# A graph network's edge counts: summed in PSUM banks per 16 targets and copied out by ScalarE, with differences at the end, and four smaller rearrangements

## What is computed

```
# layer 0: attention over edges, 8 relations, 4 heads
e = leaky_relu(el + er); alpha = softmax of e over the edges of a target
h = segment_sum(alpha * feat_src_e, edge_dst) + h_bias
# layer 1: two relations, messages depend on source node and relation alone
agg = segment_sum(edge_nn(S, W_rel[rel], b_rel[rel]), dst)
c = sigmoid(i) * tanh(g); hn = sigmoid(o) * tanh(c); three dense layers
# layer 2: two mean aggregations over the same edges
aggr = segment_sum(xp[src], dst) / max(cnt, 1)
# layer 3: for node n, the first 1875 edges' ends
out = softmax over heads of alpha(row[n], col[n]), times xt[col[n]], summed over heads
```

## Time and profile before

| | |
|---|---|
| median of three runs | 2126.85 us (2119.39 to 2128.66) |
| the profiled execution's own time | 2116.86 us |
| its span in the profile | 2115.1 us |
| PE busy | 1475.9 us (70%) |
| DVE busy | 1249.3 us (59%) |
| ACT busy | 666.2 us (31%) |
| POOL busy | 543.2 us (26%) |
| mean DMA rate | 106 GB/s |

### The profile page before, as it was taken

One profiled execution on the slowest core, in us unless ns is written; L12 is line 12 of the kernel. 1 busy time (PEld: TensorE's weight loads), 2 busy tenths in 40 slices (PEclk: granted clock), 3 DMA queues, 4 the chain that ended last, 5 costly groups with the idle time before them and its releaser, 6 DMA issues.

```text
span 2115.1 us, 20437 instructions
## 1 busy us (share of the span) xinstructions
PE 1475.9 (70%) x5426; PEld 764.4 (36%) x5426; DVE 1249.3 (59%) x2926; ACT 666.2 (31%) x1118; POOL 543.2 (26%) x517
## 2 busy tenths in 40 slices
PE   6598988677766565304777775989976589889630
PEld 3254654111111111103555554544433254644520
DVE  5221222889998888687666676520036677576705
ACT  1024764677665555200000000357732110010010
POOL 0003774677777777300000000000000000000031
PEclk9797556555555555555999998989987579999865
DMA  5924664465565565502677772000000000000021
GB/s 197 64 106 152 195 208 132 128 196 182 182 197 185 191 195 184 159 0 91 192 207 207 204 208 86 1 22 1 1 1 0 30 1 1 1 1 2 10 65 49
DMA packets 98133, 223.84 MB, mean 106 GB/s; under 512 B 32984, under 2 KB 57476, under 8 KB 97540
## 3 DMA queue, kind: packets, MB, share of 16 engines
q1 hardware_dynamic: 74084, 158.00, 23.8%
q0 software_dynamic: 23968, 64.77, 11.6%
HBM read 140.09 MB, written 82.63 MB: 105 GB/s over the span
## 4 chain that ended last, share of the span: by engine, by line
PE 48%; DVE 21%; issue 12%; POOL 12%; DMA 3%; DVEq 2%; ACT 1%; SPq 1%; POOLq 0%; ACTq 0%
PE bank L1580 14%; POOL arena L497 10%; PE bank L1519 10%; PE bank L1397 5%; DVE adjacency L936 5%; PE bank L1430 3%; PE bank L1416 3%; DVE arena L1193 2%; DVE arena L1001 2%; PE bank L1646 2%; PE bank L1564 1%; PE bank L1643 1%; SPq L363 1%; PE bank L1548 1%; DVE arena L930 1%
## 5 line engine op out<-in xcount | busy, mean ns | idle before, releaser
L497 POOL DMA_INDIRECT arena<-feat_table,arena x469 | 506.8, 1081 | 300.0 <-issue 138.3
L1467 PE MATMUL bank<-arena 128*128 128x480 f16 x586 | 319.6, 565 | 176.2 <-DVE arena L930 125.2
L565 ACT ACTIVATE arena<-bank 128x480 uint16<-128x480 f32 x586 | 307.9, 586 | 85.1 <-PE bank L1467 82.7
L505 POOL DMA_INDIRECT arena<-al_table,edge_ends x15 | 14.1, 942 | 1168.0 <-DMA al_table<-arena 1163.7
L1580 PE MATMUL bank<-arena 128*128 128x472 f16 x1440 | 294.3, 368 | 9.9 <-DVE arena L1151 5.9
L1519 PE MATMUL bank<-arena 128*128 x966 | 225.9, 387 | 83.1 <-issue 83.0
L936 DVE TENSOR_TENSOR adjacency<-adjacency,arena 128x480 uint16 x586 | 234.9, 401 | 23.4 <-ACT arena L565 16.7
L1519 PEld LDWEIGHTS bank<-arena 128*128 128x128 f32 x966 | 180.1, 191 | 129.2 <-issue 106.7
L1467 PEld LDWEIGHTS bank<-arena 128*128 128x128 f16 x586 | 60.7, 104 | 435.2 <-DVE arena L930 272.0
L930 DVE TENSOR_SCALAR arena<-iota,arena 128x480 f16<-128x480 f16 x586 | 201.5, 344 | 0.0
L1580 PEld LDWEIGHTS bank<-arena 128*128 128x128 bf16 x1440 | 142.6, 99 | 161.7 <-issue 15.5
(11 more groups left out here) (273 smaller groups left out, 1565.7 us busy)
## 6 DMA issues: line engine op xcount, KB each, us to landing
edge_rows<-arena SPq DMA_DIRECT2D x67, 910.0 KB, 4.1
arena<-edge_rows SPq DMA_DIRECT2D x117, 520.0 KB, 4.0
feat_table<-arena SPq DMA_DIRECT2D x60, 256.0 KB, 2.3
arena<-feat_table,arena POOLq DMA_INDIRECT x469
arena<-in_w SPq DMA_DIRECT2D x1, 2048.0 KB, 9.7
arena<-in_xT SPq DMA_DIRECT2D x1, 1920.0 KB, 18.5
arena<-in_x SPq DMA_DIRECT2D x1, 1792.0 KB
xt_table<-arena SPq DMA_DIRECT2D x3, 528.0 KB, 3.3
```

The lines of the kernel that those rows point to most:

```text
L497: g.indirect_dma_start(out=SLOT[k][:, j, :], out_offset=None, in_=feat_t, in_offset=bass.IndirectOffsetOnAxis(ap=IE[:, GB * b + j:GB * b + ...
L565: a.activation(EV[st % AS].rearrange("p r k -> p (r k)"), PS[4 + st % 4][:, 0:R2 * KW], ACT.Copy)\
L1467: mm(PS[4 + st % 4][:, 0:R2 * KW], OHS[st % AS], OHK[st % AS], start=True, stop=True).then_inc(s["a_mm"], 1)
```

## The change

**Counts.** `ADJ` is no longer zeroed, and DVE no longer adds. Each of four banks is cleared once, and the counts of window w accumulate in bank 4 + w mod 4 on top of what windows w-4, w-8, ... left there. ACT copies, before each step, the bank of the window before the step's to that window of `ADJ`, so that its last copy holds the window's running sum. After the last step DVE subtracts window w-4 from window w, in 29 operations of 4 windows. The evacuation has both addresses in registers, loaded 32 values at a time per 16 steps from a new table `ETAB` that DVE makes before the edge scores, and it waits for its own predecessor. PE takes its bank from registers too, loaded 32 values per 32 steps. DVE makes the source one-hots for eight steps in one operation.

```diff
-            def a_evac(i, st):
-                act.wait_ge(s["a_mm"], i * AU + (st + 1))
-                a.activation(EV[st % AS].rearrange("p r k -> p (r k)"), PS[4 + st % 4][:, 0:R2 * KW], ACT.Copy)\
+            def a_evac(st, bank, off):
+
+                act.wait_ge(s["a_mm"], max(st, 1))
+                if st:
+                    act.wait_ge(s["a_ev"], st)
+                a.activation(ADJ[:, :, bass.ds(off, KW)], BANKS[:, bass.ds(bank, R2 * KW)].rearrange("p (r k) -> p r k", r=R2), ACT.Copy)\
                  .then_inc(s["a_ev"], 1)
...
+            for st in range(STEPS):
+                if st % 16 == 0:
+                    both_ = offsets(ACTE, 2 * st, 32, KW * (WINS - 1), ETABf)
...
+                a_evac(st, banks[st % 16], offs[st % 16])
+                due = min(GC_ER + (NGB - 1 - GC_ER - GC_LATE) * (st + 1 - AS) // (STEPS - AS), NGB)
+                while got < due:
+                    collect(got)
+                    got += 1
+            a_evac(STEPS, 512 * (4 + (WINS - 1) % 4), KW * (WINS - 1))
...
-                v.tensor_scalar(OHS[st % AS], iota128[:, :], lo, None, ALU.is_equal)
+            def rows_of(st, n, lo):
+
+                v.tensor_tensor(OHS[st // AS % 2][:, 0:n, :], iota128[:, :].rearrange("p (a j) -> p a j", a=1).to_broadcast([P, n, P]),
+                                lo.rearrange("p (s a) -> p s a", a=1).to_broadcast([P, n, P]), ALU.is_equal).then_inc(s["a_rows"], 1)
...
-                v.tensor_tensor(dst, dst, EV[st % AS], ALU.add).then_inc(s["a_add"], 1)
...
+            dve.wait_ge(s["a_ev"], STEPS + 1)
+            for lo in range((WINS - 1) // 4 * 4 * KW, 0, -4 * KW):
+                n = min(4 * KW, WINS * KW - lo)
+                link(v.tensor_tensor(ADJ[:, :, lo:lo + n], ADJ[:, :, lo:lo + n], ADJ[:, :, lo - 4 * KW:lo - 4 * KW + n], ALU.subtract))
...
-                if st >= 4:
-                    pe.wait_ge(s["a_ev"], i * AU + (st - 3))
-                mm(PS[4 + st % 4][:, 0:R2 * KW], OHS[st % AS], OHK[st % AS], start=True, stop=True).then_inc(s["a_mm"], 1)
-
+                if st >= 3:
+                    pe.wait_ge(s["a_ev"], i * AU + (st - 2))
+                mm(BANKS[:, bass.ds(bank, R2 * KW)], OHS[st // AS % 2][:, st % AS, :], OHK[st % AS], start=False, stop=False,
+                   skip_group_check=True).then_inc(s["a_mm"], 1)
```

```diff
             for st in range(RSTEPS):
+                if st % RK == 0:
+                    both_ = offsets(PE, 2 * st, 2 * RK, (RRING - 1) * FW, RTABf)
...
                 if st % RG == 0:
                     pe.wait_ge(s["r_oh"], st // RG + 1)
-                    n = min(RG, RSTEPS - st)
-                    outs = offsets(PE, st, n, (NT - 1) * D, RTAB[:, 0, :])
-                    rows = offsets(PE, st, n, (RRING - 1) * FW, RTAB[:, 1, :])
```

```diff
+            dve.wait_ge(s["chunk_ready"], SH)
+            link(v.tensor_tensor(ADJ[:, 0, :], ADJ[:, 0, :], ADJ[:, 1, :], ALU.add))
+            link(v.tensor_reduce(CNTX, ADJ[:, 0, :].rearrange("p (n s) -> p n s", s=SH), AX.X, ALU.add))
+            dve.wait_ge(s["chunk_used"], R2 * SH)
+            v.tensor_copy(CNTS, CNTX).then_inc(s["cnt_red"], 1)
...
-                v.tensor_reduce(CNTS[:, n0:n1], ADJ[:, :, SH * n0:SH * n1].rearrange("p r (n s) -> p n r s", s=SH), AX.XY, ALU.add)\
-                 .then_inc(s["cnt_red"], 1)
...
                     for t in range(NT):
                         act.wait_ge(s["p_mm"], NT * v + t + 1)
                         message(t, t % 4, wide)
+                        if t in (6, 10):
+                            cast((t - 6) // 4)
+                    for c in range(2, SH):
+                        cast(c)
```

```diff
+            gates(0)
             for c in range(NC):
...
+                if c + 1 < NC:
+                    gates(c + 1)
                 pe.wait_ge(s["hn_ready"], c + 1)
```

```diff
+            for q, (t0, t1) in enumerate(GROUPS):
+                n = t1 - t0
+                dve.wait_ge(g3[q], 16 * 2 * n)
```

More of the change, by code:

```diff
@@ L83 @@
 ORING = 3
[L84 removed]
+RK = 2 * RG
+RKG = -(-RSTEPS // RK)
 assert NT <= RRING - RB and RRING % RB == 0 and RG == 2 * RB
@@ L240, in build @@
         DJR = ar(A_DJR, RSTEPS)
-        RTAB = AR[:, A_TB:A_TB + RSTRIDE].bitcast(U16).rearrange('p (two s) -> p two s', two=2)
+        RTABf = AR[:, A_TB:A_TB + RK * RKG].bitcast(U16)
+        RTAB = RTABf.rearrange('p (g two s) -> p g two s', two=2, s=RK)
         HB = ar(A_HB, D)
@@ L320, in build, with offsets @@
         f_done = [sem(f"rows_loaded{i}") for i in range(NRB)]
+        g3 = [sem(f"rows_gathered{i}") for i in range(len(GROUPS))]
         r_st = [sem(f"rows_stored{i}") for i in range(NSLOT)]
-        def offsets(engine, step, n, most, table=OFF):
+        def offsets(engine, step, n, most, table):
             return nc.values_load_multi_w_load_instructions(
@@ L669, in messages2, with cast @@
                 def messages2(wide):
+                    def cast(c):
+                        if c >= 2:
+                            act.wait_ge(s["chunk_used"], (R2 + v) * SH + c - 1)
+                        a.activation(chunk(CH2, c % 2, wide), ADJ[:, 0, :].rearrange("p (n s) -> p n s", s=SH)[:, :, c],
+                                     ACT.Copy).then_inc(s["chunk_ready"], 1)
                     for t in range(NT):
@@ L870, in _ @@
             link(v.tensor_single_scalar(IDI, IDI, RRING - 1, ALU.bitwise_and))
-            v.tensor_scalar(RTAB[:, 0, 0:RSTEPS], WSR, float(D), None, ALU.mult)
-            v.tensor_scalar(RTAB[:, 1, 0:RSTEPS], IDI, float(FW), None, ALU.mult).then_inc(s["steps_done"], 1)
+            full = RSTEPS // RK
+            rest_ = RSTEPS - RK * full
+            for j, (values, size) in enumerate(((WSR, D), (IDI, FW))):
+                v.tensor_scalar(RTAB[:, 0:full, j, :], values[:, 0:RK * full].rearrange("p (g s) -> p g s", s=RK), float(size), None, ALU.mult)
+                ins = v.tensor_scalar(RTAB[:, full, j, 0:rest_], values[:, RK * full:RSTEPS], float(size), None, ALU.mult)
+            ins.then_inc(s["steps_done"], 1)
             for c in range(SC):
@@ L1282, in _ @@
[L1282 to L1290 removed]
+            a3 = lambda j, t0, t1: S3[:, j, H * t0:H * t1].rearrange("p (t h) -> p t h", h=H)
@@ L1511, in _ @@
             for st in range(RSTEPS):
+                if st % RK == 0:
+                    both_ = offsets(PE, 2 * st, 2 * RK, (RRING - 1) * FW, RTABf)
+                    outs = [nc.s_assert_within(v, 0, (NT - 1) * D, skip_runtime_bounds_check_because="a tile number times its width") for v in both_[0:RK]]
+                    rows = both_[RK:2 * RK]
                 if st % RG == 0:
                     pe.wait_ge(s["r_oh"], st // RG + 1)
-                    n = min(RG, RSTEPS - st)
-                    outs = offsets(PE, st, n, (NT - 1) * D, RTAB[:, 0, :])
-                    rows = offsets(PE, st, n, (RRING - 1) * FW, RTAB[:, 1, :])
                 if st % RB == 0 and st < TILES:
                     pe.wait_ge(s["r_wgt"], st // RB + 1)
-                mm(BANKS[:, bass.ds(outs[st % RG], D)], OHR[:, (st // RG) % ORING, P * (st % RG):P * (st % RG + 1)],
-                   FBf[:, bass.ds(rows[st % RG], D)], start=False, stop=False, skip_group_check=True).then_inc(s["r_mm"], 1)
+                mm(BANKS[:, bass.ds(outs[st % RK], D)], OHR[:, (st // RG) % ORING, P * (st % RG):P * (st % RG + 1)],
+                   FBf[:, bass.ds(rows[st % RK], D)], start=False, stop=False, skip_group_check=True).then_inc(s["r_mm"], 1)
             pe.wait_ge(s["ht_add"], 8)
```

231 lines of the change are left out of this document (119 added, 112 removed).

## The result

| | median | runs | ratio (95% interval) |
|---|---|---|---|
| kernel before, beside it | 2127.76 us | 4, 2119.39 to 2144.0 | |
| changed kernel | 2511.82 us | 4, 2510.76 to 2512.43 | 1.179 (1.172 to 1.186) |
| predicted | 2059 us, 1970 to 2155 | | |

What follows compares the result with a forecast made beforehand. DVE's counting and POOL's gathers bound the counts together; the change moves the bound to ACT. 0 + 71 - 70 - 52 + 2 - 3 - 16 = -68 on 2116.86 gives 2049, median 10 above: 2059 us, range 1970 to 2155.

Steps and rivals of the forecast that it cites:

- I take 2.1: Count loop: ACT's load of 32 16-bit values per 16 steps was taken as 2.1 us; 37 loads add 57 us.
- rival A: 16-bit loads cost by the value, 7.5 us per 32: +200 in counts, rows +52 instead of -70; 2381 us; chance 0.17.
- The step itself: Count loop: one ACT evacuation awaiting its predecessor takes 0.57 us plus a 0.19 gap, 0.76; bounds 0.47 and 0.87.
- the free collects: Count loop: the 44 collects between ACT's steps add some 0.1 us each, 4 us.
- the gathers left at the end: After the last evacuation: ACT's collects pace POOL, leaving 49 gathers, 68 us; last gather at 943 against 871.65, +71 us.
- Rival B: Count loop: waiting for the own predecessor is almost free, 0.57 us a step; 1953 us; chance 0.10.
- three steps just cover PE's own load: Count loop: PE is three steps ahead, 2.3 us, which just covers its own load of 2.1 us.
- One load of 2.1 us per 16 steps hides wholly: Rows: PE's single load is fully hidden, so PE alone would need 3.5 to 3.7 us per 8 steps instead of 5.16.
- mixture of three: Rows: PE, DVE and loads with weighing all meet near 3.7 us per 8 steps; taken as 4.05, -70 us.
- The result (-52 against -54): Gates: PE alternates gates and dense layers without a pause, 81 us from 1551 to 1633; -52 us.
- layer 2: Layer 2: of 14 us for `both` before the messages, -3 us is kept because of ACT's casts; bounds -14 and +4.
- The tail: Tail: DVE starts groups of tiles before the last gather, 11 us a group, ending at 2090; -16 us, bounds -21 and -8.

## Why the prediction was wrong

**The step that failed** is "A load of 32 (32-bit) values took DVE 2.10 us, of 20 values took PE 1.37. I take 2.1". The nearest row was chosen by the number of values; the right one was nearest by type. The two 16-bit rows (1.92 for 8, 0.754 for 3, no fixed part) were read and priced at 0.233 us a value in rival A, which got a chance of 0.17. They were the only rows of the table's own kind, and this price was right: 0.235 measured on PE, and 0.211, a tenth less, on ACT.

**Counts.** The step itself (0.76 us), the start, the free collects and the gathers left at the end (68 us worked out, 61.5 measured) were right. Rival B had 0.57 us a step where 0.757 was measured: in the tail of the kernel before an engine did go on 0.02 to 0.03 us after the other (DVE's line 1109 to ACT's 595 and back to DVE's 1111), but in this loop, with the addresses from registers, ACT stood 0.19 us between two evacuations. With 2.1 us a load the loop would be 531 instead of 506 us, since the sentence that three steps just cover PE's own load was too hopeful. With the loads as they are it is 807. Rival A had +200 for ACT's loads, and they cost 245 - 61 = 184 more than cheap ones (169 by the run with PE's table alone in 16 bits); what it left out is PE's own loads, 105 us against 25 with cheap ones.

**Rows.** "One load of 2.1 us per 16 steps hides wholly" failed in the same way. Rival A's 12 us per 16 steps were 13.6: it kept PE's products at the old speed, and at a granted clock of 0.76 a product took 482 ns on average, where it takes 387 in the kernel before and 386 with the 32-bit table. No rival had the clock of the rows in it. With cheap loads the rows are 233 to 238 us, a little under the 239 of the working, and the bound is PE itself (212.73 of 222 us), no mixture of three. A small slip besides: 61 groups at 5.16 - 4.05 us are 68 us, not 70.

**Gates.** The result (-52 against -54) was right, with a granted clock of 0.91 where it had been 0.72, and the sum on DVE was named as what holds each chunk. That the gain is of neither edit alone was not seen; by the chain it could have been: 9.6 us of gates against 11.8 of the sum.

**Sums, layer 2, tail.** Within 5 us each; layer 2 gained nothing (+1 in place of -3). The tail gave 20 where 16 were expected: a group of four tiles costs DVE 10.7 us with its round trips, and DVE stands 34.7 us for the first gathers in place of 61.9.

**The rest of the sum.** From measured stages: 2512 - (807 - 531) - (411 - 233) = 2058 us. So the forecast of 2059 is about what the change would do with 32-bit tables on the first kind of chip, where that version was not run; the run with PE's table alone in 16 bits gives it by another way, 2159.8 - 107 = 2053. That the first sum comes within 1 us is luck: 25 us too little for the loop and 4 for layer 2 are made up by 21 too much elsewhere (6.5 for the last gathers, 6 for the rows, 3.5 for the tail, 3 for the start, 2 for the gates) and by the 10 us added for the median, which in the changed kernel lies 0.3 us above the profiled execution. The price by the value that was set against the change, 0.233 us, held for the 16-bit loads of these kernels (0.21 to 0.28 by the medians of their stages) and for none of the 32-bit ones (0.06 to 0.09).

What was not tried: 16-bit values packed in pairs into 32-bit words and taken apart in registers, and whether 16-bit loads cost the same on DVE or SyncE. That the type and not the place of a table makes its loads cheap is shown for `ETAB`, which begins at the same word in both types (6.75 us for 32 values against 1.97); `RTAB` and `PBANK` moved when they became wider, and the 16-bit `PBANK` stayed dear at a second address.

## What to carry to other kernels

When a trace has two prices for one operation, take the row that matches in data type and engine before the one that matches in size, and price the whole change by the other row too; here one row decided 450 us. Hold tables that registers are loaded from in 32 bits: this edit alone took 77 us, 3.6%, out of the kernel before by the traces (4.6% by the medians, which hold the count loop's own variation). When a pause on PE grows, look at the granted clock too: here the slower products cost 71 us and the longer pauses 31. Before overlapping a step, look in the chain of waits whether it is on it; an edit that buys nothing alone can be worth 20 us once its neighbour is gone.

## What the runs showed of the hardware

- The register loads took longer with every value, and with 16-bit values over three times as long, for 8 values as for 32: 16 bits 0.754 us for 3, 1.92 for 8, 7.53 for 32 on PE, 6.75 for 32 on ACT; 32 bits 0.588 us for 8, 1.37 for 20, 2.13 for 32 on PE, 1.97 for 32 on ACT. In the rows PE's loads of one size agree within 0.06 us (7.52 to 7.57); in the counts the medians of its loads of 32 are 7.54 to 8.93 us (16 bits) and 2.38 to 2.71 (32 bits), and single ones last up to 9.4 and 4.1.
- With PE pausing 3.8 us once per 16 steps in the rows, the granted clock was 0.76 and a product took 482 ns; with 1.45 us once per 8 steps it was 0.97 and 387 ns, and with 9 us of pauses in the whole stage of 232 it was 1.00 and 387 ns.
- The same program took 2138 and 2145 us on two chips and 2268 and 2272 on two others. In the traces from the slower two with the old count loop ACT pauses up to 4.5 us at "issue" in the counts and PE up to 4.1; in those from the faster two ACT has no such pause and PE none above 0.2 us. Why is open.
